# Type one-hots of the first relational layer: from one DVE compare to two ACT passes, in a two-layer graph kernel on one core

## The reference

```python
c = comp[etype]
for b in range(num_bases):
    xb = h @ V[b]
    m = m + c[:, b, None] * xb[src]
m = m * norm
agg = jax.ops.segment_sum(m, dst, num_segments=h.shape[0])
out = agg + bias + h @ loop_w
```

## Time and profile before

| | |
|---|---|
| median of 3 runs | 2055.03 us (2051.82 to 2055.29) |
| the profiled execution, its own time | 2051.85 us |
| its span, first to last instruction | 2050.1 us |
| mean granted TensorE clock | 0.894 |
| PE busy | 1695.4 us (83%) |
| DVE busy | 1398.6 us (68%) |
| ACT busy | 356.9 us (17%) |
| POOL busy | 1401.6 us (68%) |

### The profile page before, as it was taken

The page is one execution under the profiler, slowest core; times in us unless marked ns, Lnnn a source line. Parts: engine busy times, 40 slices in busy tenths (PEclk is TensorE's granted clock), DMA queues, the critical chain, the costliest instruction groups (busy, mean ns, idle before and its releaser), DMA issues. The chain is left out here.

```text
span 2050.1 us, 40639 instructions
## 1 busy us (share of the span) xinstructions
PE 1695.4 (83%) x12305; PEld 1222.6 (60%) x12306; DVE 1398.6 (68%) x2294; ACT 356.9 (17%) x869; POOL 1401.6 (68%) x1527
## 2 busy tenths in 40 slices
PE   1488888888888888888579888889999899968998
PEld 1366656556656656566457666666666666755564
DVE  7887887787887887787677666666566657511443
ACT  2032222222222222222101011010110111101300
POOL 5777777777777777777277777777777777777000
PEclk8589889989889899989789899999999999968999
DMA  5334334434334334333222222233233332334463
GB/s 147 92 95 113 99 95 106 98 89 110 98 88 111 98 89 111 96 95 90 57 58 64 57 61 60 57 83 101 80 89 84 82 97 77 91 93 127 146 231 121
DMA packets 194039, 196.66 MB, mean 96 GB/s; under 512 B 109132, under 2 KB 157273, under 8 KB 193946
## 3 DMA queue, kind: packets, MB, share of 16 engines
q0 software_dynamic: 45760, 93.81, 18.3%
q1 hardware_dynamic: 140134, 97.59, 16.6%
q10 hardware_dynamic: 8052, 4.04, 0.7%
HBM read 169.75 MB, written 25.57 MB: 95 GB/s over the span
## 5 line engine op out<-in xcount | busy, mean ns | idle before, releaser
L811 POOL DMA_INDIRECT ring<-h_rows,rel_idx x1312 | 1255.9, 957 | 401.1 <-issue 370.4
L982 DVE TENSOR_TENSOR rel_pick<-rel_src_row,dve_bank 128x1664 bf16<-128x1664 int32 (+1 forms) x268 | 485.7, 1813 | 184.4 <-PE rel_ps_p L1211 85.6
L1280 PE MATMUL rel_ps_z<-rel_C,ring 128*128 128x56 f32 x3100 | 418.7, 284 | 192.0 <-DVE ring L988 101.9
L1280 PEld LDWEIGHTS rel_ps_z<-rel_C,ring 128*128 128x128 f32 x3100 | 401.2, 201 | 242.6 <-issue 232.2
L1378 ACT ACTIVATE rel_ZT<-rel_ps_z 128x304 f32 x292 | 114.2, 426 | 1109.3 <-PE rel_ps_z L1280 1107.7
L1224 PE MATMUL rel_ps_p<-rel_h_parts,rel_pick 128*128 128x384 bf16 x1150 | 266.6, 362 | 0.0
L1368 ACT ACTIVATE rel_A<-rel_ps_a 128x500 f32 x292 | 165.5, 603 | 368.0 <-PE rel_ps_a L1168 212.4
L1211 PE MATMUL rel_ps_p<-rel_h_parts,rel_pick 128*128 128x384 bf16 x1100 | 196.6, 338 | 22.0 <-DVE rel_h_parts L970 22.0
L1211 PE MATMUL carried<-rel_h_parts,rel_pick 128*128 128x384 bf16 x1100 | 194.9, 336 | 2.4 <-DVE rel_pick L982 2.4
L1168 PE MATMUL rel_ps_a<-rel_M,rel_lo 128*128 128x175 bf16 x784 | 154.7, 302 | 24.9 <-DVE rel_M L949 24.9
L1211 PEld LDWEIGHTS rel_ps_p<-rel_h_parts,rel_pick 128*128 128x128 bf16 x1100 | 111.3, 103 | 96.5 <-issue 33.7
(11 more groups left out here) (232 smaller groups left out, 1711.8 us busy)
## 6 DMA issues: line engine op xcount, KB each, us to landing
ring<-h_rows,rel_idx POOLq DMA_INDIRECT x1312
A_slabs<-rel_A SPq DMA_DIRECT2D x25, 800.0 KB
A_slot<-A_slabs SPq DMA_DIRECT2D x25, 800.0 KB, 4.5
rel_types<-edge_types SPq DMA_DIRECT2D x97, 200.0 KB
early_slot<-A_slabs SPq DMA_DIRECT2D x18, 896.0 KB, 6.0
rel_src_row<-in_src_dram SPq DMA_DIRECT2D x134, 64.0 KB, 3.2
last_slot<-A_slabs SPq DMA_DIRECT2D x4, 512.0 KB, 5.9
ring<-h_rows,idx_table POOLq DMA_INDIRECT x118
```

Source lines behind the costliest of these rows:

```text
L811: g_.indirect_dma_start(ring[:, s * CHUNK + i, :], None, rows_in, bass.IndirectOffsetOnAxis(ap=idx[which][:, n:n + 1], axis=0)).then_inc(l ...
L982: v.tensor_tensor(pick[:, b0:b0 + n, :], src_row[s][:, :].unsqueeze(1).to_broadcast(shape), node_ids[:, b0:b0 + n].unsqueeze(2).to_broadca ...
L1280: ins = m_.matmul(bank(ps_z[s], NB)[:, :, bass.ds(at[i], TW)], ring[:, first + i, :], C[s][:, i, :, :], start=False, stop=(i == n - 1))
```

## The change

ACT makes the layer-0 one-hots, in two passes over each half: the square of (type - p), with the bias -p from a new column table, written into the one-hot buffer, and then relu(1 - square) in place. For whole numbers this is 1 where the type is p and 0 elsewhere. A semaphore of ACT's own stands between the passes. In the loop the four passes stand behind both slab copies of the chunk and ahead of `spread`. DVE's compares go, in the prologue too. On PE the degree product of j = 3 moves from behind the second picked part to right behind the slab, ahead of the product that waits for the one-hots. Two small constants are added: a column of ones (POOL) and the negated types (DVE, in the preparation).

```diff
@@ prepare
             io_(t.group_lo[:, :], [[P, GROUPS]])
+            g.memset(t.one_col[:, :], 1.0).then_inc(consts_set, 1)
...
             dve.wait_ge(comp_in, 64)
+            v.tensor_scalar(t.less_type[:, :], t.type_id[0:RH, :], -1.0, None, ALU.mult)
@@ class Coefficients
+    def square_and_turn(self, act, m, quarter_m, s, h):
+
+        if h == 0:
+            after(act, self.product_done, m - 1)
+            act.wait_ge(self.etype_in[s], (quarter_m + 1) * 16)
+        ins = self.onehot[:, s % 2, h, :]
+        self.nc.scalar.activation(ins, self.etype[:, s % 2, :], ACT.Square, bias=self.t.less_type[:, h:h + 1]).then_inc(self.squared, 1)
+        act.wait_ge(self.squared, 2 * m + (h + 1))
+        made = self.nc.scalar.activation(ins, ins, ACT.Relu, bias=self.t.one_col[:, 0:1], scale=-1.0)
+        if h == 1:
+            made.then_inc(self.onehot_ready, 1)
@@ relational_layer, DVE
-                for m in range(AHEAD):
-                    co.make_onehot(dve, m, m // 4, m % 4)
-                    if m:
-                        co.scale(dve, m - 1, m - 1)
+                for m in range(AHEAD - 1):
+                    co.scale(dve, m, m)
...
-                    if makes(g, j):
-                        co.make_onehot(dve, c + AHEAD, g + (j + AHEAD) // 4, (j + AHEAD) % 4)
@@ relational_layer, PE
                     if layer == 0:
                         sum_slab(c, j % 2, at)
+                    if layer == 0 and j == 3 and not is_first:
+                        degrees(g - 1)
...
-                    if layer == 0 and j == 3 and not is_first:
-                        degrees(g - 1)
                     s, n = sum_edges(g, c, j, at)
@@ relational_layer, ACT
+            for m in range(AHEAD if layer == 0 else 0):
+                for h in range(2):
+                    co.square_and_turn(act, m, m // 4, m % 4, h)
...
                         spread_slab(g, j, parity, at[4:6], 1)
                     if layer == 1 and j == 0 and not (isinstance(g, int) and g < 2):
                         fin.act_hnT(act, g - 2)
+                    for h in range(2 if makes(g, j) else 0):
+                        co.square_and_turn(act, c + AHEAD, g + (j + AHEAD) // 4, (j + AHEAD) % 4, h)
                     spread(g, j, parity, at, s)
```

More of the change, by code:

```diff
@@ L340, in _ @@
             k.link(v.tensor_reduce(t_min[:, :], dst_f[:, :, :], AX.X, ALU.min))
-            dve.wait_ge(consts_set, 19)
+            dve.wait_ge(consts_set, 20)
             cols = [P, RAW, P]
@@ L457, in __init__ @@
         self.summed, self.sum_ready = ctx.enter_context(nc.sbuf_tensor(f"{name}_summed", [P, ET, 2 * NB], F32)), sem("sum_ready")
+        self.squared = sem("squared")
         self.onehot_ready, self.product_done, self.coef_ready = sem("onehot_ready"), sem("product_done"), sem("coef_ready")
@@ L1983, in program @@
         t.comp = sb("comp_parts", [RH, 2, 3, 2 * NB], BF16)
+        t.less_type, t.one_col = sb("less_type", [RH, 2], F32), sb("one_col", [RH, 1], F32)
         t.group_lo = sb("group_lo", [P, GROUPS], F32)
```

## The result

The changed kernel takes 2662.33 us median (6 runs, 2654.16 to 2669.56), the kernel before 2053.54 us (6 runs, 2046.9 to 2055.29): ratio 1.2974, 95% interval 1.2955 to 1.2992. The forecast was 2565 us, with a range of 2430 to 2700. The profiled execution of after has a span of 2667.6 us, against 2050.1.

What follows compares the result with a forecast made beforehand. POOL's gathers were taken as the bound, 9.55 us a chunk. Prologue +11, chunks 0 to 3 +14 and chunks 4 to 91 +488 (15.1 us each) gave +513 on 2051.85: 2565 us, range 2430 to 2700.

Steps and rivals of the forecast that it cites:

- closed loop: Chunks 0 to 91: ACT's passes wait for PE's slab of the same chunk, PE's product for them; 15.1 us a chunk.
- The start: Prologue and chunks 0 to 3: +11 us for six one-hots made by ACT, +14 us for four longer chunks.
- Slab to one-hots ready: First part of a chunk, from PE's slab to the end of ACT's passes; mean 8.0 us at the high clock.
- this is 7.3 us for j = 1 and 2: Slab start to one-hots ready: 2.54 us to the second copy's end, 0.1 to get going, 4.65 for passes.
- the slab runs high: PE's slab in each loop chunk was taken at the high clock, 1.25 us; twice that at the low clock.
- Product to slab: PE's work from one-hots ready to the next slab: 5.1 us low, then 2.0 us high; 8.9 us if all low.
- I take the mean of the two low times, 5.1 us, at the start of each burst: PE's work behind the product: low clock for 5.1 us, mean of 3.4 and 6.9, doing 57% of it.
- rival 2: PE's clock stays low as in the start: 17.6 us a chunk, +733, 2785 us; chance 0.10.
- Prices nothing: Moving PE's degree product of j = 3 adds nothing beyond the 9.0 us from slab to one-hots at j = 3.
- 1 (clock high, 2354 us): PE's clock recovers at once or never falls: 12.7 us a chunk, +302, 2354 us; chance 0.10.
- 3 (hidden, about 2040 us): One-hots ready when PE comes, POOL stays the bound, its gathers lose their stretch: about 2040 us; chance 0.03.
- 4 (table switches): Square needs another ACT function table; two loads a chunk add 2.6 us, +226, 2790 us; chance 0.04.

Runs made afterwards that it cites:

- E6: Changed kernel with ACT's four passes ahead of the two slab copies instead of behind them; 2348.15 us, ratio 1.1435 to the kernel before.
- E7: Changed kernel with ACT making one-hots of chunk c + 7, PE still multiplying c + 6, on the faster chip; 2033.02 us, ratio 0.9899 to the kernel before.
- E11: Changed kernel without the two relu passes of each chunk, on the slower chip; 2752.56 us, ratio 1.0844 to the kernel before.
- E8: Changed kernel with 20 matmuls of zeros on PE ahead of each chunk's wait for one-hots, faster chip; 2494.71 us, ratio 1.2148 to the kernel before.
- E2: Kernel before with only the degree product of j = 3 moved right behind the slab, slower chip; 2521.62 us, ratio 0.9825 to the kernel before.
- E9: Same kernel as E2, run again on the slower chip; 2508.74 us, ratio 0.987 to the kernel before.
- E1: Same kernel as E7, on the slower chip; 2528.66 us, ratio 0.9842 to the kernel before.
- E4: Same kernel as E8, on the slower chip; 2981.23 us in its one run, 1.160 of the kernel before.

## Why the prediction was right, and which terms were mis-sized

**Bound and mechanism.** Right. The closed loop slab, copies, passes, product, edge sums was the cause (E6, E7; E11 for the passes in it), POOL lost its place as the bound, and layer 1 and the dense stages stayed as they were (-4.1 us behind chunk 91). "PE's product waits about 6 us for ACT's relu in some 90 chunks": 5.48 us in 88. "The granted clock of the stretch near 0.7": 0.64.

**The passes.** 1.13 us forecast, 1.135 and 1.147 measured; the chain 4.65 forecast, 4.54 measured. The gap between square and relu that I bounded at up to 0.3 us is not there: the relu's row starts 1.17 us after that of a square of 1.13.

**The start.** +25 us forecast, +24.7 measured. In it PE's products come 4.44 us apart (65.30, 69.74 and 74.18 us), one set of passes each.

**The chunk: 15.1 us forecast, 16.33 measured.** This is where nearly all of the 104 us between the two increases (513 and 617.5 us) lies: 88 x 1.23 = 108 us. Both of its terms were too small.

*Slab to one-hots ready*, 8.0 us forecast; slab to product is 8.69, so +0.69 us a chunk, 61 us. By j (0 to 3) the forecast was 8.2, 7.3, 7.3, 9.0; measured 8.96, 7.05, 8.77, 9.96. Two steps failed. The first is "this is 7.3 us for j = 1 and 2". I had read it from a chunk with j = 1. At j = 2 ACT's first slab copy starts 2.74 us after the slab and not 1.0, because ACT comes from the output of the group (H and its store, 698.52 to 699.37 in the timeline above) and begins the copy 1.66 us later. PE's first half of the slab is done 0.26 us into that time (699.63), and for the rest the profile shows nothing; ACT's program has there the loading of the chunk's column numbers, which isn't counted as busy, and no run tested that. The kernel before already had it: 2.89 us at j = 2 and 1.92 at j = 0 against 0.98 at j = 1, over the same 80 chunks. Reading j = 2 there as well would have closed 1.5 / 4 = 0.37 of the 0.69 us, and reading j = 0, where the copy in after starts at 1.97, another 0.19. The second is "the slab runs high", which was given without a row. The slab is at the low clock over its first 1.3 us in 58 of the 80 chunks. That costs at j = 3, where ACT's first copy waits for the degree product behind it: the copy starts 2.96 us after the slab and not 1.80. E8 has both clocks at j = 3, and slab to product is 8.96 us in the 8 chunks with the slab at the high clock and 9.94 in the 12 with a low one. In the mean over j this is about 0.24 us a chunk; j = 1 and the rounding to 8.0 gave 0.1 back.

*Product to slab*, 7.1 us forecast (5.1 us low, then 2.0 high), 7.64 measured, +0.54 us a chunk, 48 us. The step that failed is "I take the mean of the two low times, 5.1 us, at the start of each burst". Two errors of opposite sign met. The low clock did not end after 5.1 us: the whole burst shown above is low, and so are 56 of the 60 bursts with j = 1, 2 and 3 in chunks 8 to 87; their means are 6.87, 6.83 and 7.08 us. The nearer assumption was rival 2's. But its price for an all-low burst, 8.9 us with and 7.4 without the output, was too high: without the output it is 6.9. Only at j = 0, where the output comes in between, does a burst take 9.76 us, less than the 13.4 of an all-low one (7.4, and 4 x 1.5 for the output): there the clock is low for about the first half in 16 of 20, which is the 5.1 us that I had given to all four. Of the 16.33 us the share of the way from all high (12.7) to all low (17.6) is 74%; I had 49%.

**Who waits on POOL.** Forecast was the shared edge, "5 us a chunk". The amount was right, the place not: 452.0 us, 5.14 a chunk, are the half-way wait for the type product, and the shared edge has 143.1, 1.6 a chunk.

**The degree product.** "Prices nothing" holds inside this change, where ACT's lateness hides all else. As a part by itself it is worth more than a per cent on the slower chip (E2, E9), by the wait of ACT's first copy that I had read in the rows and priced only for the changed kernel.

**The rivals.** 1 (clock high, 2354 us) is out; E8 shows that even with PE kept busy the chunk is 14.33 and not 12.7, as slab to product is 8.61 and product to slab 5.80 instead of 4.7. 2 (clock low, 2785 us) was right about three of four bursts and too dear in its price for them. 3 (hidden, about 2040 us) did not come; E7 reaches a like time, 2033 us, with one more chunk of lead, but not by shorter gathers, as its last gather starts when that of the kernel before does. 4 (table switches) is out, one load in the trace.

The total lies inside the range because the loop was right. That the start came out to 0.3 us is not luck (chunk 0's first slab matmuls 10.3 us later, 11 forecast; chunks 0 to 3 14.3 us longer, 14 forecast), but in the bursts a wrong length of the low time and a wrong price of it took part of each other away.

## What to carry to other kernels

A lead of six chunks covers nothing if the instruction that makes the data stands, on its own engine, behind a wait for the current chunk: follow the chain of releases round once, and if it closes within one turn, its length becomes the length of the turn. To move work to an idle engine, look at where in that engine's order it stands and at who waits for it, more than at its duration: the same four passes cost 606, 294 or nothing, in us of the total, by their place in the order or one more chunk of lead. And what PE does behind such a wait has a second price: here, with 5.5 us of waiting in each turn, three of four bursts ran at the low clock from end to end.

## What the runs showed of the hardware that I had not expected

The same program takes 2054 us on one chip and 2539 to 2570 us on another, at a single core. The difference is there in every kernel run on both (E1 and E7, E4 and E8). Single instructions of ACT and POOL are as long on both: ACT's passes take 1135 and 1148 ns and a gather 955 ns, in E1 as in E7. In the slower chip's rows PE has idle time put down to "issue", with nothing that the profile shows behind it; for the kernel of E9, from 110 to 1150 us, in us in all, times and longest:

```profile
PE rel_ps_z L1280 <- issue: 81.0, 115, 1.9
PE rel_ps_p L1224 <- issue: 38.0, 34, 2.5
PE rel_ps L482 <- issue: 24.0, 29, 2.0
```

In the kernel before on the faster chip the first of these groups has 0.3 us. The granted clock is lower there too: 0.80 over the kernel before against 0.89. What holds PE up there is open. One of E1's six runs took 8651.77 us; nothing in the others shows why.

A low clock cost time only where PE was the one waited for. In E8 the clock of the loop went from 0.64 to 0.92, and slab to product changed by 0.08 us in the mean. What change there was stands at j = 3, where ACT waits for a product of PE behind the slab: there slab to product took 9.94 us behind a slab at the low clock, and 8.96 behind one at the high clock.
